# Two recurrences of a convolutional LSTM chain: who rounds the state and who multiplies by the forget gate

## The chip, the cores and the metric

One Trainium2 chip, one of its cores. The metric is the device time of one execution of the whole program in microseconds (us); lower is better. Three executions of the kernel before took 2058.46, 2059.15 and 2060.22 us, median 2059.15.

## What is computed

The input x is 8 images of 48 channels, 64 x 64. Four layers follow one another: an axial filter with attention (L0), two layers of a ConvLSTM that scans the image by rows in both directions (L1, L2), and an inverted residual (L3). The change touches only the scans of L1 and L2. Cut to what matters, one such layer is:

```python
def step(carry, xr):
    h, c = carry
    inp = jnp.concatenate([xr, h], axis=1)
    gates = lax.conv_general_dilated(inp, w_mid, (1,), 'SAME', dimension_numbers=dn) + b[None, :, None]
    i, f, g, o = jnp.split(gates, 4, axis=1)
    c2 = jax.nn.sigmoid(f) * c + jax.nn.sigmoid(i) * jnp.tanh(g)
    h2 = jax.nn.sigmoid(o) * jnp.tanh(c2)
    return ((h2, c2), h2)
hs_f = scan(step, rows)            # 64 rows of 8 x 48 x 64
hs_b = scan(step, rows, reverse=True)
# then: projection of both, batch norm over everything, relu, + x
```

## The kernel before

`build` runs the four layers one after the other; `lstm_scans` is called twice, once for each recurrence. Both directions of a scan are carried in the same tiles, on different partitions: direction d has its own 48 channels (of i and g, and of the state h) on the partitions from `near[d]`, and those of f, o and the cell from `far[d]`, where near and far are 0 and 64 or the other way round. One row of an image batch is 48 channels by BW = 512 columns (8 images of 64). A *turn* below is one direction of one row; a step `s` has two turns, d = 0 and d = 1, and while one direction's gates are computed on the tensor engine, the other's are worked off by the other engines.

The convolution is 14 matmuls of 128 x 112 x 512 for a turn (`chunk`, L712), in two accumulations: `ps[d][0]` holds i and f, `ps[d][1]` g and o. The operands are fp32r, which is rounded, so each of x and h is split into a rounded high part (HI) and the rest (LO). The first two matmuls take part of x (`xc`), the next six x's low part and the high part of h (`xh[..., HI, :]`), the last six the low part of h and a high part.

Each engine has its program written out by hand, and semaphores join them. Nothing plans or reorders. In one turn:

- ScalarE: sigmoid of i and f (L769); then `state_hi` for the other direction, which rounds the new state to the HI part in two halves of 256 columns, each as soon as VectorE has written it (`h_full`, L749); tanh of g in place in PSUM (L773); `copy_state`, the whole state into the LO tile of the other partitions (L756); sigmoid of o (L776); and the tanh of the cell in two halves (L779).
- VectorE: `keep` = sigmoid(f) * cell (L827), i * g in place in PSUM (L830), cell = keep + i*g (L834), the state `hs` = sigmoid(o) * tanh(cell) in two halves (L841), and after direction 1 the rounding of a later row of x (`split_hi`, L819).
- GpSimd: `split_lo`, the low part of x (L685), and `state_lo`, the low part of the state (L676), which waits for `h_hi`. Both are 48 x 512.
- PE waits for `h_hi` ahead of the middle six matmuls and for `h_copy` and `h_lo` ahead of the last six.
- SyncE only issues DMAs: loads of rows of x and their spreading over partitions.

`cell`, `tanh_c` and the gates lie in PSUM; `gate_if`, `gate_o`, `keep`, `hs`, `xh` and `xs` in SBUF. GpSimd reads and writes SBUF tiles only.

Of the kernel before, what the change touches and what calls it, by code (L numbers as in the profile page):

```python
# [13 lines left out]
P = 128  # L14
HALF = 64
HB = B // 2
# [516 lines left out]
def lstm_scans(nc, D, hs, rows_in, weights, tag):  # L533
# [12 lines left out]
    with ctx:  # L546
# [3 lines left out]
        def sb(name, shape, dt=F32):  # L550
            return ctx.enter_context(nc.sbuf_tensor(name + tag, shape, dt))
# [18 lines left out]
        begun = sb("begun", [P, 10])  # L570


        cell = ctx.enter_context(nc.psum_tensor("cell" + tag, [P, BW], F32))
# [17 lines left out]
        kept = [sem(f"kept{d}") for d in range(2)]  # L591
        added = [sem(f"added{d}") for d in range(2)]
        cells = [sem(f"cells{d}") for d in range(2)]
        h_hi = [sem(f"h_hi{d}") for d in range(2)]
# [10 lines left out]
        def inner(ap):  # L605

            return padded(ap)[:, :, 1:W + 1]

        def wide(ap):

            return ap.rearrange("p (b w) -> p b w", b=B)

# [4 lines left out]
        with nc.Block() as block:  # L617
# [49 lines left out]
            @block.gpsimd  # L667
            def _(pool):
                pool.memset(xs[:, :, :].bitcast(F32), 0.0).then_inc(cleared, 1)

                def state_lo(t, row, d, s):

                    n = near[d]
                    pool.wait_ge(h_hi[d], t + 2)
                    whole = hs[n:n + C, bass.ds(row, 1), :].rearrange("p a (b w) -> p (a b) w", b=B)
                    pool.tensor_tensor(inner(xh[n:n + C, d, 1 - s, LO, :]), whole,  # L676
                                       inner(xh[n:n + C, d, 1 - s, HI, :]).bitcast(F32), ALU.subtract).then_inc(h_lo[d], 1)

                def split_lo(t, d, s):

                    f = far[d]
                    pool.wait_ge(x_hi, t + 1)
                    if not (isinstance(t, int) and t < 2):
                        pool.wait_ge(gates[d][1], t - 1)
                    pool.tensor_tensor(inner(xh[f:f + C, d, s, HI, :]), wide(xf[f:f + C, s, :]),  # L685
                                       inner(x_rows(s, slice(f, f + C))).bitcast(F32), ALU.subtract).then_inc(x_lo[d], 1)
                pool.wait_ge(cleared, 3)
                pool.wait_ge(xf_cleared, 1)
                for s in range(2):
                    for d in range(2):  # L690
                        split_lo(s, d, s)

                def step(k, last=False):
                    for s in range(2):
                        for d in range(2):
                            if not last:
                                split_lo(2 * k + (s + 2), d, s)
                            if not last or s == 0:
                                state_lo(2 * k + s, 2 * k + s if d == 0 else k * -2 + (H - 1 - s), d, s)
                with pool.Fori(0, H // 2 - 1) as k:  # L700
                    step(k)
                step(H // 2 - 1, last=True)

            @block.tensor
            def _(pe):
                pe.wait_ge(w_ready, 4)
                pe.wait_ge(cleared, 3)
                with pe.Fori(0, H // 2) as k:
                    for s in range(2):
                        for d in range(2):  # L710
# [11 lines left out]
                            pe.wait_ge(h_hi[d], 2 * k + (s + 1))  # L722
# [11 lines left out]
            def _(act):  # L734
                act.wait_ge(cleared, 3)
                for d in range(2):
                    act.wait_ge(h_hi[d], 1)
                    act.wait_ge(cells[d], 1)
# [5 lines left out]
                def state_hi(t, row, d, s):  # L744

                    n = near[d]
                    for j, part in enumerate(parts):
                        act.wait_ge(h_full[d], t * 2 + (j + 1))
                        hi = nc.scalar.activation(padded(xh[n:n + C, d, s, HI, :])[:, j * HB:(j + 1) * HB, 1:W + 1],  # L749
                                                  state(row, d)[:, part].rearrange("p (b w) -> p b w", b=HB), ACT.Copy)  # L750
                    hi.then_inc(h_hi[d], 1)
# [6 lines left out]
                def step(k, first=False, last=False):  # L758
                    for s in range(2):
                        for d in range(2):  # L760
# [9 lines left out]
                            if some:  # L770
                                state_hi(earlier, row, 1 - d, slot)
                            act.wait_ge(gates[d][1], 2 * k + (s + 1))
# [14 lines left out]
            def _(dve):  # L787
# [19 lines left out]
                for d in range(2):  # L807
                    for i, first in enumerate((h_hi[d], h_lo[d], h_copy[d], sig_if[d], sig_o[d])):
                        nc.vector.memset(begun[:, 5 * d + i:5 * d + i + 1], 0.0).then_inc(first, 1)
# [11 lines left out]
                def step(k, more=2):  # L821
                    for s in range(2):
                        for d in range(2):
# [3 lines left out]
                            nc.vector.tensor_tensor(keep[n:n + C, :], gate_if[f:f + C, d, :], cell[f:f + C, :],  # L827
                                                    ALU.mult).then_inc(kept[d], 1)
# [3 lines left out]
                            dve.wait_ge(kept[d], 2 * k + (s + 1))  # L832
                            dve.wait_ge(added[d], 2 * k + (s + 1))
                            nc.vector.tensor_tensor(cell[f:f + C, :], keep[n:n + C, :], ps[d][1][n:n + C, :], ALU.add  # L834
                                                    ).then_inc(cells[d], 1)
                            dve.wait_ge(sig_o[d], 2 * k + (s + 2))
# [6 lines left out]
                        if s < more:  # L843
                            split_hi(2 * k + (s + 3), 1 - s)
# [5 lines left out]
                step(H // 2 - 1, more=0)  # L850
# [732 lines left out]
```

## Time and profile before

| | us |
|---|---|
| median of three executions | 2059.15 |
| lowest, highest | 2058.46, 2060.22 |
| the profiled execution, its own time | 2065.48 |
| its span in the profile | 2063.5 |
| PE, ScalarE (ACT), VectorE (DVE), GpSimd (POOL) busy | 1656.2, 1198.6, 1257.3, 637.5 |
| first and last keep product (L827) of the two recurrences | 297.2, 1470.6 |

How to read it: a profile is one execution, with the busy time of each engine, the groups of instructions by line with what ended the idle time before them, and a timeline. PE is the tensor engine's matmuls and PEld its weight loads, ACT is ScalarE, DVE is VectorE, POOL is GpSimd, SP is SyncE. In a row, `out<-in` names the tiles, and a name such as `xh_l` stands for the tile of both recurrences. PEclk is the clock that was granted to the tensor engine as a share of its full speed. The busy time of an engine counts over stages that have different limits, so the recurrences are read on their own.

### The profile page before, as it was taken

How to read it: one execution, taken by the hardware profiler on the slowest of the kernel's cores; microseconds unless marked ns; L12 is line 12 of the kernel's file. 1: busy time of each engine (PE TensorE's matmuls, PEld its weight loads, DVE VectorE, ACT ScalarE, POOL GpSimd, SP SyncE). 2: the span in 40 equal slices, each digit the busy share in tenths (PEclk: the TensorE clock that was granted, in tenths of full speed). 3: DMA queues.
4: the chain of work that ended last, by engine and by line, in shares of the span. 5: the costliest groups of instructions: out<-in, count | busy, mean ns of one | idle time of the engine just before them, and what ended most of it. 6: DMA issues, size and time to landing. Idle time of an engine off the chain costs nothing. (4 is left out here: it accounts for less than half of the span.)

```text
span 2063.5 us, 45378 instructions
## 1 busy us (share of the span) xinstructions
PE 1656.2 (80%) x15282; PEld 993.8 (48%) x15282; DVE 1257.3 (61%) x2182; ACT 1198.6 (58%) x2461; POOL 637.5 (31%) x577
## 2 busy tenths in 40 slices
PE   6979238888888887606888888888726999999999
PEld 5545125555555555204555555555403455555555
DVE  5538957777777777455777777777664233333334
ACT  1115218888888888345888888888661232222220
POOL 2010025555555554204555555555200000000000
PEclk9989669999999999757999999999966999999999
DMA  1769356666666664855767776776492001110100
GB/s 62 253 202 216 97 125 105 106 107 105 106 106 106 106 106 68 137 164 95 106 106 106 106 107 105 106 106 107 68 192 53 18 19 32 33 33 18 33 18 26
DMA packets 132283, 199.69 MB, mean 97 GB/s; under 512 B 28528, under 2 KB 47824, under 8 KB 131920
## 3 DMA queue, kind: packets, MB, share of 16 engines
q1 hardware_dynamic: 132176, 198.08, 52.0%
q8 instruction: 89, 1.46, 0.3%
q14 instruction: 18, 0.15, 0.0%
HBM read 73.72 MB, written 37.75 MB: 54 GB/s over the span
## 5 line engine op out<-in xcount | busy, mean ns | idle before, releaser
L712 PE MATMUL gates_l<-xh_l,w_l 128*112 128x512 f32 x3072 | 796.2, 408 | 138.4 <-ACT xh_l L749 138.4
L712 PEld LDWEIGHTS gates_l<-xh_l,w_l 128*112 128x112 f32 x3072 | 511.6, 176 | 423.4 <-issue 285.4
L676 POOL TENSOR_TENSOR xh_l<-hs,xh_l 48x512 fp32r<-48x512 f32 x252 | 301.3, 1196 | 453.1 <-ACT xh_l L749 453.1
L685 POOL TENSOR_TENSOR xh_l<-xf_l,xs_l 48x512 fp32r<-48x512 f32 x256 | 306.0, 1195 | 47.5 <-DVE xs_l L819 47.0
L1259 PE MATMUL b_dw<-b_hid,b_diag 32*32 32x512 f32 x9120 | 313.7, 601 | 0.0
L841 DVE TENSOR_TENSOR hs<-gate_o_l,tanh_c_l 48x256 f32 (+1 forms) x512 | 193.2, 416 | 146.4 <-ACT tanh_c_l L779 146.4
L712 PE MATMUL gates_l<-xc_l,w_l 128*112 128x512 f32 x512 | 165.0, 404 | 144.9 <-DMA xc_l<-xs_l 138.5
L1259 PEld LDWEIGHTS b_dw<-b_hid,b_diag 32*32 32x32 f32 x9120 | 188.0, 103 | 114.4 <-issue 47.4
L830 DVE TENSOR_TENSOR gates_l<-gate_if_l,gates_l 48x512 f32<-48x512 f32 x256 | 178.1, 696 | 87.9 <-ACT gates_l L773 84.0
L779 ACT ACTIVATE tanh_c_l<-cell_l 48x256 f32<-48x256 f32 x512 | 158.1, 342 | 104.7 <-DVE cell_l L834 104.7
L769 ACT ACTIVATE gate_if_l<-gates_l 112x512 f32<-112x512 f32 x256 | 151.2, 590 | 105.2 <-PE gates_l L712 102.0
L1327 ACT ACTIVATE b_h<-b_dw,b_bias_r 128x512 f32<-128x512 f32 x64 | 40.5, 684 | 284.8 <-PE b_dw L1259 284.8
L834 DVE TENSOR_TENSOR cell_l<-keep_l,gates_l 48x512 f32<-48x512 f32 x256 | 178.3, 696 | 26.7
L749 ACT ACTIVATE xh_l<-hs 48x256 fp32r (+1 forms) x504 | 181.6, 407 | 7.9
L827 DVE TENSOR_TENSOR keep_l<-gate_if_l,cell_l 48x512 f32<-48x512 f32 x256 | 175.4, 685 | 10.7 <-ACT gate_if_l L769 1.6
L1371 DVE TENSOR_SCALAR b_h<-b_dw,b_bias_r 128x512 f32<-128x512 f32 x64 | 45.1, 747 | 220.2 <-PE b_dw L1259 220.2
L712 PEld LDWEIGHTS gates_l<-xc_l,w_l 128*112 128x112 f32 x512 | 89.6, 176 | 178.4 <-issue 146.2
L756 ACT ACTIVATE xh_l<-hs 48x512 fp32r (+1 forms) x252 | 159.1, 631 | 6.1
L776 ACT ACTIVATE gate_o_l<-gates_l 48x512 f32<-48x512 f32 x256 | 151.9, 593 | 6.2
L773 ACT ACTIVATE gates_l<-gates_l 48x512 f32<-48x512 f32 x256 | 145.7, 569 | 3.2
L1321 ACT ACTIVATE b_hid<-b_ex,b_bias_h 128x512 f32<-128x512 f32 x116 | 73.8, 689 | 87.6 <-PE b_ex L1231 87.6
L1231 PE MATMUL b_ex<-b_xs,b_w1s 48*128 48x512 f32 x240 | 72.1, 679 | 54.5 <-DMA b_xs<-rows 50.3
(146 smaller groups left out, 1289.5 us busy)
## 6 DMA issues: line engine op xcount, KB each, us to landing
xc_l<-xs_l SPq DMA_DIRECT2D x512, 99.0 KB, 3.0
xh_l<-xs_l SPq DMA_DIRECT2D x512, 66.0 KB, 2.4
xf_l<-rows SPq DMA_DIRECT2D x256, 96.0 KB, 2.1
hs<-rows SPq DMA_DIRECT2D x32, 384.0 KB, 10.2
rows<-hs SPq DMA_DIRECT2D x32, 384.0 KB, 4.9
xr<-in_x_rows SPq DMA_DIRECT2D x24, 256.0 KB, 2.7
xc<-in_x_cols SPq DMA_DIRECT2D x24, 256.0 KB, 2.9
mixed<-stage SPq DMA_DIRECT2D x24, 256.0 KB, 3.0
```

Source lines behind the costliest of these rows:

```text
L676: pool.tensor_tensor(inner(xh[n:n + C, d, 1 - s, LO, :]), whole, inner(xh[n:n + C, d, 1 - s, HI, :]).bitcast(F32), ALU.subtract).then_inc( ...
L685: pool.tensor_tensor(inner(xh[f:f + C, d, s, HI, :]), wide(xf[f:f + C, s, :]), inner(x_rows(s, slice(f, f + C))).bitcast(F32), ALU.subtrac ...
L712: return nc.tensor.matmul(ps[d][m][0:K, :], w[:, d, q, m, :], padded(tile)[:, :, lo:lo + W], start=first, stop=last)
L749: hi = nc.scalar.activation(padded(xh[n:n + C, d, s, HI, :])[:, j * HB:(j + 1) * HB, 1:W + 1], state(row, d)[:, part].rearrange("p (b w) - ...
L756: nc.scalar.activation(inner(xh[f:f + C, d, s, LO, :]), wide(state(row, d)), ACT.Copy).then_inc(h_copy[d], 1)
L776: nc.scalar.activation(gate_o[f:f + C, d, :], ps[d][1][f:f + C, :], ACT.Sigmoid).then_inc(sig_o[d], 1)
L779: nc.scalar.activation(tanh_c[f:f + C, j, 0:PART], cell[f:f + C, part], ACT.Tanh).then_inc(tanhs[d], 1)
L827: nc.vector.tensor_tensor(keep[n:n + C, :], gate_if[f:f + C, d, :], cell[f:f + C, :], ALU.mult).then_inc(kept[d], 1)
L830: nc.vector.tensor_tensor(ps[d][1][n:n + C, :], gate_if[n:n + C, d, :], ps[d][1][n:n + C, :], ALU.mult).then_inc(added[d], 1)
L834: nc.vector.tensor_tensor(cell[f:f + C, :], keep[n:n + C, :], ps[d][1][n:n + C, :], ALU.add).then_inc(cells[d], 1)
L841: nc.vector.tensor_tensor(whole[:, part], gate_o[f:f + C, d, part], tanh_c[f:f + C, j, 0:PART], ALU.mult).then_inc(h_full[d], 1)
L1259: mm = nc.tensor.matmul(dw[r][j * Q:(j + 1) * Q, :], diag[i * Q:(i + 1) * Q, g, 3 * dy + 3 + dx, :], hid[g][i * Q:(i + 1) * Q, y % RING, : ...
```

## The change

Within `lstm_scans`:

- `state_hi` on ScalarE rounds only the first half of the state (`ACT_HALF`). VectorE copies the second half (`DVE_HALF`) itself, behind its two products L841, with a wait on its own result and a one-column memset ahead of the copy. `h_hi` becomes two semaphores, and who waited for one waits for both (PE, GpSimd). ScalarE waits for the second half of the state ahead of its tanh of g.
- The forget product is halved: VectorE makes the first 256 columns, GpSimd the second (`keep_cell`), placed on GpSimd between `split_lo` and `state_lo`. VectorE waits for both halves before it adds. `keep` is written on the cell's own partitions.
- `cell` moves from PSUM to SBUF.
- `split_hi` on VectorE moves: in direction 1 from behind L841 to between the cell's sum and the wait for the sigmoid of o.

```diff
         keep = sb("keep", [P, BW])
-        begun = sb("begun", [P, 10])
-
-
-        cell = ctx.enter_context(nc.psum_tensor("cell" + tag, [P, BW], F32))
+        cell = sb("cell", [P, BW])
+        begun = sb("begun", [P, 13])
...
                 def state_lo(t, row, d, s):
 
                     n = near[d]
-                    pool.wait_ge(h_hi[d], t + 2)
+                    pool.wait_ge(h_hi[d][0], t + 2)
+                    pool.wait_ge(h_hi[d][1], t + 2)
                     whole = hs[n:n + C, bass.ds(row, 1), :].rearrange("p a (b w) -> p (a b) w", b=B)
                     pool.tensor_tensor(inner(xh[n:n + C, d, 1 - s, LO, :]), whole,
                                        inner(xh[n:n + C, d, 1 - s, HI, :]).bitcast(F32), ALU.subtract).then_inc(h_lo[d], 1)
+
+                def keep_cell(t, d):
+
+                    f = far[d]
+                    pool.wait_ge(sig_if[d], t + 2)
+                    pool.wait_ge(cells[d], t + 1)
+                    pool.tensor_tensor(keep[f:f + C, parts[1]], gate_if[f:f + C, d, parts[1]], cell[f:f + C, parts[1]],
+                                       ALU.mult).then_inc(kept[d][1], 1)
...
+                keep_cell(0, 0)
 
                 def step(k, last=False):
                     for s in range(2):
                         for d in range(2):
                             if not last:
                                 split_lo(2 * k + (s + 2), d, s)
+                            if not (last and s == d == 1):
+                                keep_cell(2 * k + (s + d), 1 - d)
...
-                            pe.wait_ge(h_hi[d], 2 * k + (s + 1))
+                            pe.wait_ge(h_hi[d][0], 2 * k + (s + 1))
+                            pe.wait_ge(h_hi[d][1], 2 * k + (s + 1))
...
-                    for j, part in enumerate(parts):
-                        act.wait_ge(h_full[d], t * 2 + (j + 1))
-                        hi = nc.scalar.activation(padded(xh[n:n + C, d, s, HI, :])[:, j * HB:(j + 1) * HB, 1:W + 1],
-                                                  state(row, d)[:, part].rearrange("p (b w) -> p b w", b=HB), ACT.Copy)
-                    hi.then_inc(h_hi[d], 1)
+                    act.wait_ge(h_full[d], t * 2 + 1)
+                    nc.scalar.activation(half(xh[n:n + C, d, s, HI, :], ACT_HALF), state(row, d)[:, parts[ACT_HALF]].rearrange("p (b w) -> p b w", b=HB),
+                                         ACT.Copy).then_inc(h_hi[d][ACT_HALF], 1)
...
+                            if some:
+                                act.wait_ge(h_full[1 - d], earlier * 2 + 2)
...
                         for d in range(2):
                             n, f = near[d], far[d]
                             dve.wait_ge(sig_if[d], 2 * k + (s + 2))
                             dve.wait_ge(cells[d], 2 * k + (s + 1))
-                            nc.vector.tensor_tensor(keep[n:n + C, :], gate_if[f:f + C, d, :], cell[f:f + C, :],
-                                                    ALU.mult).then_inc(kept[d], 1)
+                            nc.vector.tensor_tensor(keep[f:f + C, parts[0]], gate_if[f:f + C, d, parts[0]], cell[f:f + C, parts[0]],
+                                                    ALU.mult).then_inc(kept[d][0], 1)
                             dve.wait_ge(tanh_g[d], 2 * k + (s + 1))
                             nc.vector.tensor_tensor(ps[d][1][n:n + C, :], gate_if[n:n + C, d, :], ps[d][1][n:n + C, :],
                                                     ALU.mult).then_inc(added[d], 1)
-                            dve.wait_ge(kept[d], 2 * k + (s + 1))
+                            for j in range(2):
+                                dve.wait_ge(kept[d][j], 2 * k + (s + 1))
                             dve.wait_ge(added[d], 2 * k + (s + 1))
-                            nc.vector.tensor_tensor(cell[f:f + C, :], keep[n:n + C, :], ps[d][1][n:n + C, :], ALU.add
+                            nc.vector.tensor_tensor(cell[f:f + C, :], keep[f:f + C, :], ps[d][1][n:n + C, :], ALU.add
                                                     ).then_inc(cells[d], 1)
+                            if d == 1 and s < more:
+                                split_hi(2 * k + (s + 3), 1 - s)
...
-                        if s < more:
-                            split_hi(2 * k + (s + 3), 1 - s)
+                            if not (last and s == 1):
+                                dve.wait_ge(h_full[d], 4 * k + (2 * s + DVE_HALF + 1))
+                                nc.vector.memset(begun[:, 12:13], 0.0)
+                                nc.vector.tensor_copy(half(xh[n:n + C, d, 1 - s, HI, :], DVE_HALF), whole[:, parts[DVE_HALF]].rearrange("p (b w) -> p b w", b=HB)
+                                                      ).then_inc(h_hi[d][DVE_HALF], 1)
```

The diff is cut to its core; left out are semaphore lists and `half(ap, j)`, which takes half j of the 8 images of a padded tile. Where code is written in another order, two places show it. On GpSimd, the body of its loop over rows, first half (`split_lo` and `state_lo` write `xh`; `ISA` and `REGISTER_ALU` are waits and address arithmetic). Before:

```order
L684 REGISTER_ALU
L685 TENSOR_TENSOR xh_l<-xf_l,xs_l 48x8x64
L674 REGISTER_ALU
L676 ISA
L676 TENSOR_TENSOR xh_l<-hs,xh_l 48x8x64
L685 TENSOR_TENSOR xh_l<-xf_l,xs_l 48x8x64
L676 ISA
L676 TENSOR_TENSOR xh_l<-hs,xh_l 48x8x64
```

and with the change:

```order
L699 REGISTER_ALU
L700 TENSOR_TENSOR xh_l<-xf_l,xs_l 48x8x64
L689 REGISTER_ALU
L691 TENSOR_TENSOR keep_l<-gate_if_l,cell_l 48x256
L683 ISA
L683 TENSOR_TENSOR xh_l<-hs,xh_l 48x8x64
L700 TENSOR_TENSOR xh_l<-xf_l,xs_l 48x8x64
L691 TENSOR_TENSOR keep_l<-gate_if_l,cell_l 48x256
L683 ISA
L683 TENSOR_TENSOR xh_l<-hs,xh_l 48x8x64
```

One instruction of 256 columns now stands ahead of each `state_lo`. On VectorE, direction 1 at the end of its loop body, from the forget product on (`xs` is the rounded row of x). Before:

```order
L827 TENSOR_TENSOR keep_l<-gate_if_l,cell_l 48x512
L830 TENSOR_TENSOR gates_l<-gate_if_l,gates_l 48x512
L834 TENSOR_TENSOR cell_l<-keep_l,gates_l 48x512
L841 ISA
L841 TENSOR_TENSOR hs<-gate_o_l,tanh_c_l 48x256
L841 ISA
L841 TENSOR_TENSOR hs<-gate_o_l,tanh_c_l 48x256
L813 ISA
L817 REGISTER_ALU
L819 CAST xs_l<-xf_l 112x8x64
```

and with the change:

```order
L846 TENSOR_TENSOR keep_l<-gate_if_l,cell_l 48x256
L849 TENSOR_TENSOR gates_l<-gate_if_l,gates_l 48x512
L854 TENSOR_TENSOR cell_l<-keep_l,gates_l 48x512
L832 ISA
L836 REGISTER_ALU
L838 CAST xs_l<-xf_l 112x8x64
L863 ISA
L863 TENSOR_TENSOR hs<-gate_o_l,tanh_c_l 48x256
L863 ISA
L863 TENSOR_TENSOR hs<-gate_o_l,tanh_c_l 48x256
L867 MEMSET begun_l 128x1
L868 COPY xh_l<-hs 48x4x64
```

The CAST of x stands ahead of the two products that write `hs`, no longer behind them, and a memset and a copy into `xh` follow them.

## Rows read from the trace of the kernel before

**Rows 1.** The page's totals: busy us (share of the span) xinstructions, by engine.
```profile
PE 1656.2 (80%) x15282; PEld 993.8 (48%) x15282; DVE 1257.3 (61%) x2182; ACT 1198.6 (58%) x2461; POOL 637.5 (31%) x577
```

**Rows 2.** Windows, 400 to 800 us: busy us (xinstructions) of each engine, then clock and DMA.
```profile
core 0: us, PE busy (x) PEld busy (x) DVE busy (x) ACT busy (x) POOL busy (x), PEclk, DMA share, GB/s
400.00:800.00 400.00, 346.06 (x1361) 226.06 (x1360) 295.60 (x534) 353.85 (x779) 228.38 (x195) 1.00 0.69 106
```

**Rows 3.** Groups in 400 to 800 us: busy us, mean ns | idle before, releaser.
```profile
L841 DVE TENSOR_TENSOR hs<-gate_o_l,tanh_c_l 48x256 f32 x192 | 72.4, 416 | 55.4 <-ACT tanh_c_l L779 55.4
...
L834 DVE TENSOR_TENSOR cell_l<-keep_l,gates_l 48x512 f32<-48x512 f32 x97 | 67.6, 697 | 10.1
...
L827 DVE TENSOR_TENSOR keep_l<-gate_if_l,cell_l 48x512 f32<-48x512 f32 x97 | 66.4, 685 | 3.6
...
L756 ACT ACTIVATE xh_l<-hs 48x512 fp32r x97 | 61.2, 631 | 2.3
L779 ACT ACTIVATE tanh_c_l<-cell_l 48x256 f32<-48x256 f32 x196 | 60.5, 342 | 36.4 <-DVE cell_l L834 36.4
...
L776 ACT ACTIVATE gate_o_l<-gates_l 48x512 f32<-48x512 f32 x97 | 57.6, 594 | 2.4
```

**Rows 4.** Timeline from 799 us: start, us, engine, line, operation [idle before <-releaser].
```profile
799.77 0.58 ACT L769 ACTIVATE gate_if_l<-gates_l 112x512 f32<-112x512 f32 x1
...
800.38 0.72 ACT L749 ACTIVATE xh_l<-hs 48x256 fp32r x2
800.45 0.43 DVE L819 CAST xs_l<-xf_l 112x512 fp32r<-112x512 f32 x1
...
801.00 0.57 ACT L773 ACTIVATE gates_l<-gates_l 48x512 f32<-48x512 f32 x1
...
801.30 1.19 POOL L676 TENSOR_TENSOR xh_l<-hs,xh_l 48x512 fp32r<-48x512 f32 x1 [1.70 <-ACT xh_l L749]
...
803.80 0.60 ACT L769 ACTIVATE gate_if_l<-gates_l 112x512 f32<-112x512 f32 x1
...
804.42 0.72 ACT L749 ACTIVATE xh_l<-hs 48x256 fp32r x2
...
805.17 0.57 ACT L773 ACTIVATE gates_l<-gates_l 48x512 f32<-48x512 f32 x1
...
805.29 3.11 PE L712 MATMUL gates_l<-xh_l,w_l 128*112 128x512 f32 x12 [0.48 <-ACT xh_l L749]
805.33 1.19 POOL L676 TENSOR_TENSOR xh_l<-hs,xh_l 48x512 fp32r<-48x512 f32 x1 [1.68 <-ACT xh_l L749]
...
805.77 0.70 DVE L830 TENSOR_TENSOR gates_l<-gate_if_l,gates_l 48x512 f32<-48x512 f32 x1 [0.66 <-ACT gates_l L773]
...
806.58 0.70 DVE L834 TENSOR_TENSOR cell_l<-keep_l,gates_l 48x512 f32<-48x512 f32 x1
...
807.31 0.61 ACT L779 ACTIVATE tanh_c_l<-cell_l 48x256 f32<-48x256 f32 x2 [0.30 <-DVE cell_l L834]
807.76 0.74 DVE L841 TENSOR_TENSOR hs<-gate_o_l,tanh_c_l 48x256 f32<-48x256 f32 x2 [0.48 <-ACT tanh_c_l L779]
807.85 0.58 ACT L769 ACTIVATE gate_if_l<-gates_l 112x512 f32<-112x512 f32 x1
```

**Rows 5.** Single lines of VectorE: duration ns min/median/max, first and last start, forms.
```profile
L819 DVE CAST xs_l<-xf_l x128: 421/429/431, 281.0 to 1450.5; 112x512 fp32r<-112x512 f32 x128
...
L213 DVE COPY fx<-hs x96: 209/220/223, 38.0 to 127.4; 64x128 f32 x64, 64x128 f32<-64x128 f32 x32
...
L809 DVE MEMSET begun_l<- x20: 59/59/59, 280.8 to 933.1; 128x1 f32 x20
```

**Rows 6.** Timeline of GpSimd from 840 us, columns as in rows 4.
```profile
840.94 1.30 POOL L950 TENSOR_TENSOR b_diag<-b_eye,b_wds 128x288 f32<-128x288 f32 x2
```

**Rows 7.** Timeline of the program's first 17 us, GpSimd and VectorE, same columns.
```profile
1.14 13.74 POOL L157 MEMSET hs<- 32x16384 f32 x1
...
4.00 10.96 DVE L184 CAST dist<-disti 64x127 f32<-64x127 int32 x1
...
15.51 0.22 DVE L191 TENSOR_SCALAR dist<-dist 64x127 f32<-64x127 f32 x1
```

More of the change, by code:

```diff
@@ L590, in lstm_scans @@
         tanhs = [sem(f"tanhs{d}") for d in range(2)]
-        kept = [sem(f"kept{d}") for d in range(2)]
+        kept = [[sem(f"kept{d}_half{j}") for j in range(2)] for d in range(2)]
         added = [sem(f"added{d}") for d in range(2)]
         cells = [sem(f"cells{d}") for d in range(2)]
-        h_hi = [sem(f"h_hi{d}") for d in range(2)]
+        h_hi = [[sem(f"h_hi{d}_half{j}") for j in range(2)] for d in range(2)]
         h_copy = [sem(f"h_copy{d}") for d in range(2)]
@@ L611, in wide, with half @@
             return ap.rearrange("p (b w) -> p b w", b=B)
+        ACT_HALF, DVE_HALF = 0, 1
+        def half(ap, j):
+            return padded(ap)[:, j * HB:(j + 1) * HB, 1:W + 1]
         def x_rows(r, rows):
@@ L736, in _ @@
                 for d in range(2):
-                    act.wait_ge(h_hi[d], 1)
+                    act.wait_ge(h_hi[d][0], 1)
                     act.wait_ge(cells[d], 1)
@@ L807, in _ @@
                 for d in range(2):
-                    for i, first in enumerate((h_hi[d], h_lo[d], h_copy[d], sig_if[d], sig_o[d])):
-                        nc.vector.memset(begun[:, 5 * d + i:5 * d + i + 1], 0.0).then_inc(first, 1)
+                    for i, first in enumerate((*h_hi[d], h_lo[d], h_copy[d], sig_if[d], sig_o[d])):
+                        nc.vector.memset(begun[:, 6 * d + i:6 * d + i + 1], 0.0).then_inc(first, 1)
                 def split_hi(t, r):
@@ L819, in split_hi, with step @@
                     nc.vector.tensor_copy(inner(x_rows(r, slice(0, K))), wide(xf[0:K, r, :])).then_inc(x_hi, 1)
-                def step(k, more=2):
+                def step(k, more=2, last=False):
                     for s in range(2):
@@ L849, in _ @@
                 step(H // 2 - 2, more=1)
-                step(H // 2 - 1, more=0)
+                step(H // 2 - 1, more=0, last=True)
 class ResidualConstants:
```

## The prediction

> **What bounds the kernel now.** I read the page's totals first, then the two recurrences by stretch, then one stretch turn by turn. The totals say little [rows 1]: the tensor engine is busy 80% of the span, but over stages of different kinds. In a stretch of the first recurrence the clock is 1.00 of full, PE is busy 346 of 400 us, ScalarE 354, VectorE 296, GpSimd 228 [rows 2]: nobody is full. Who waits for whom tells why: ScalarE idles before the cell's tanh and always on VectorE's cell (L834), 36.4 us in 400 [rows 3], and PE idles before the matmuls on the state on ScalarE's rounding (L749), 0.48 us each time [rows 4]. That is a ring, and the timeline gives its links [rows 4]. A "turn" is one direction of one row; L819, once for two turns, has run 128 times [rows 5], so there are 256 turns, 128 in each recurrence. Take T = 803.80, the start of the sigmoid of i and f (L769). Then L749 twice from 804.42, tanh of g (L773) 805.17, product i*g (L830) 805.77, cell (L834) 806.58, tanh of the cell (L779) 807.31, next sigmoid 807.85. The links are 0.62 + 0.75 + 0.60 + 0.81 + 0.73 + 0.54 = 4.05 us. Over two turns, 799.77 to 807.85, it is 4.04, the value I use. VectorE's forget product (L827), the low half of the state on GpSimd (L676) and PE lie beside this ring.
>
> **The change, part by part, if no engine disturbs another.**
> *ScalarE* loses the second L749. The pair takes 0.62 from its start to the next ScalarE instruction in the turn at 800.38 [rows 4], so one is 0.31. The ScalarE ring becomes 4.04 - 0.31 = 3.73.
> *VectorE* gets, behind the two products L841, a wait on its own result, a 1-column memset and the copy of the second half, and its forget product shrinks to 256 columns. Its ring from one tanh of the cell to the next: from the tanh's start to the first L841 0.45 (807.31 to 807.76), plus 0.04 because the cell is now read from SBUF (the 512-column ScalarE instruction is 631 ns from SBUF to SBUF in L756 and 594 from PSUM to SBUF in L776 [rows 3]); the two L841 0.74, a wait on its own result 0.11 (L830 ends 806.47, L834 starts 806.58), the memset 0.06 [rows 5]; the copy 0.29; the half product 0.42 as L841 of the same size [rows 3], plus 0.03; then 0.81 and 0.73 as now. Sum 0.49 + 0.91 + 0.32 + 0.45 + 0.81 + 0.73 = 3.71. The copy's 0.29 has no row; 64x128 takes 220 ns and 112x512 429 [rows 5], which bracket it, and a line between them gives 0.29. The CAST of x (L819, 0.43) moves into VectorE's wait for the tanh, which is 0.45 to 0.49 long: nothing, while that wait covers it; without cover it costs 0.43 in every second turn.
> *GpSimd* gets half the forget product ahead of the low half of the state. Two instructions of 288 columns take 1.30 [rows 6], so 256 columns take 0.58. Asked for at T + 0.60 + 0.19 (GpSimd starts 0.19 after its releaser: 805.14 to 805.33), so from 0.78 to 1.36 after T; state_lo, 1.20 long, to 2.56; split_lo, as large, to 3.76. PE needs 0.15 after a release, and 2.56 from its first state matmul (805.29) to the next sigmoid (807.85), of which the first six of twelve take half of 3.11; so state_lo leads to the next sigmoid at 2.56 + 0.15 + 1.01 = 3.72.
> For VectorE's own write of the cell to SBUF I add nothing: L834 takes 697 ns into PSUM and L827, as wide, 685 into SBUF [rows 3]. PE's busy time alone is 346 of 400 us [rows 2], 3.50 of a turn of 4.04. So three rings end within 0.02 of one another, with PE's own work 0.2 below them. Undisturbed the turn is 3.73, worth 256 x 0.31 = 79 us. But nothing has slack: whatever delays VectorE or GpSimd by more than 0.02 is paid.
>
> **What speaks against it.** At the start of the program GpSimd fills a tile from 1.14 to 14.88, and VectorE's SBUF-to-SBUF CAST of 127 columns, begun at 4.00, ends at 14.96 [rows 7]. A TENSOR_SCALAR of the same 64x127, once GpSimd is idle, takes 0.22. So a VectorE copy waits for the GpSimd instruction that is running, and goes on 0.08 after it. By this the sum that I forecast from is the blocked one. The Trainium skill, page "SBUF — State Buffer", section "Who interferes with whom", says the same in general: a VectorE copy or cast in a two-port mode and a GpSimd instruction take one shared port pair for a whole instruction, and the later one fully blocks. By that rule the trace agrees with the sum below; without it the sum is the 3.73 above.
> In the kernel before, this costs nothing. L819 starts at 800.45 with GpSimd idle until 801.30 [rows 4] and takes 421 to 431 ns in all 128 cases [rows 5]. L830 runs beside state_lo (805.77 against 805.33 to 806.52) at its usual 0.70: with one operand in PSUM it is not held up.
> After the change two kinds of copies meet a busy GpSimd:
> (a) The CAST, in the turns of direction 1. VectorE asks for it once the cell is written, at 0.62 + 0.31 + 0.60 + 0.81 + 0.70 + 0.03 = 3.07 after T. GpSimd's split_lo runs from 2.56 to 3.76. The CAST then starts at 3.84, ends at 4.27, and the first L841, due at 3.07 + 0.49 = 3.56, is 0.71 late.
> (b) The copy of the state, every turn, asked for at -0.54 + 0.49 + 0.91 = 0.86 after T (the tanh starts 0.54 before T, then the terms of VectorE's ring), while GpSimd's half product is asked for at 0.78. If GpSimd is first, the copy waits until 1.44, 0.58 late. If VectorE is first, by as much as one late release, GpSimd starts at about 1.15, all its later work moves by 0.37, and the CAST of (a) becomes about 1.1 late.
> Two turns are 2 x 3.73 = 7.46. With (a) alone, 8.17: 4.09 a turn, +12 us. With (a) and VectorE first in (b), about 8.57: 4.29, +63. With (a) and GpSimd first in one of the two turns (in the turn behind the CAST, VectorE is so late that GpSimd is through), 8.75: 4.38, +87. I take 4.25, between these, as the order of (b) will not be the same throughout: 256 x (4.25 - 4.04) = **+54 us**.
> Everything outside the recurrences is unchanged: the three memsets more are 0.06 each [rows 5]. The sum is 2065.5 + 54 = 2119 for a profiled execution; the median of the runs is 2059.15, 0.3% below that execution, so I forecast 2113.
>
> **The rivals.**
> A, it is faster: GpSimd's arithmetic doesn't hold VectorE up. The row that shows the block has a GpSimd MEMSET, which only writes, for 13.74 us; L676 and L685 also compute and might hold the port only in short pieces. Against it: the CAST waited to the very end of that instruction. The turn is then 3.73, 79 us less: 1980. It decides if CAST and copy show some 0.43 and 0.29 beside a busy GpSimd.
> B, only the forget product is blocked: with the cell in SBUF its VectorE half has two SBUF operands, which no instruction in these recurrences had. It is asked for at 0.86 + 0.32 = 1.18, GpSimd's half ends at 1.36: 0.26 late with the restart, 3.97 to 4.03 a turn, 2041 to 2056. No row here has such a VectorE instruction beside GpSimd. The Trainium skill, the same page and section, states that a VectorE instruction with two SBUF inputs contends with a GpSimd instruction that reads SBUF. Under the blocked copies it would add little, since the copy ahead has waited for the same instruction.
> C, a partial block (GpSimd lets go within its instruction), which lands about halfway between 3.73 and 4.25, near 4.0 a turn: 2040 to 2075.
> DMA queues are none: their waits are all at the start, and two turns' loads keep their place and number.
>
> **How the numbers follow.** Blocked copies 0.64, its own range 2071 to 2150. A 0.16, B 0.12, C 0.08. About 0.2% (4 us) is what a measurement can tell from no change. Slower: 0.64 and 0.02 of C, 0.66. Faster: A, 0.10 of B, 0.03 of C, 0.29. Same: 0.05. The range has to reach down to A to leave out less than 2 in 10: 1976 to 2155.
>
> **What would show it.** Right: L819 after the change far over 0.43, about 1.2, in nearly every case, ending 0.08 behind a GpSimd instruction; the rounding copy at 0.29 or near 0.85 by turns; uneven turns, direction 1's late; ScalarE's wait for the cell above the 0.37 of now (36.4 us in 98 turns [rows 3]); ScalarE with one L749 a turn. Wrong: CAST at 0.43 with split_lo running through it, turns of 3.73 alike (A), or the 48x256 product alone lengthened (B). Not priced: longer turns leave PE idler than its 87% of now [rows 2]; should the granted clock fall below 1.00 within the recurrences, the matmuls would take their place in the ring.

## The result, and the profile after

| | before | with the change |
|---|---|---|
| median of five executions, us | 2060.22 | 2081.95 |
| lowest, highest | 2058.46, 2067.93 | 2079.47, 2083.66 |
| ratio over the runs, 95% interval | | 1.0087 (1.0068 to 1.0106) |
| the profiled execution, its span | 2065.48, 2063.5 | 2080.05, 2077.7 |

The kernel is slower: by 0.87%, or 18 us, by the ratio, and the two medians are 22 us apart. I had forecast slower, by 54 us. In the two profiled executions the recurrences, from their first sigmoid of i and f to their last, grew from 528.1 and 526.1 us to 538.8 and 534.2, 18.8 us together; the stretch between them happened to be 4.0 us shorter. The page of the changed kernel gives its totals and groups (line, engine, operation, tiles, count | busy us, mean ns | idle us before, releaser):

```profile
PE 1668.7 (80%) x15282; PEld 982.5 (47%) x15282; DVE 1401.6 (67%) x2690; ACT 1144.4 (55%) x2209; POOL 833.9 (40%) x833
...
L683 POOL TENSOR_TENSOR xh_l<-hs,xh_l 48x512 fp32r<-48x512 f32 x252 | 309.6, 1229 | 99.5 <-DVE xh_l L868 99.5
...
L691 POOL TENSOR_TENSOR keep_l<-gate_if_l,cell_l 48x256 f32<-48x256 f32 x256 | 187.9, 734 | 196.2 <-ACT gate_if_l L786 196.2
L798 ACT ACTIVATE tanh_c_l<-cell_l 48x256 f32<-48x256 f32 x512 | 176.5, 375 | 142.4 <-DVE cell_l L854 142.4
...
L868 DVE CAST xh_l<-hs 48x256 fp32r (+1 forms) x252 | 143.6, 570 | 3.4
```

Against [rows 1], ScalarE has lost 54 us of work, VectorE has 144 more and GpSimd 196 more, of which its half product, 734 ns each, is 188. `state_lo` (L683) now waits for VectorE's copy, no longer for ScalarE's rounding. The same stretch as [rows 2], then groups of it as in [rows 3]:

```profile
400.00:800.00 400.00, 344.71 (x1331) 217.37 (x1330) 344.27 (x713) 325.50 (x666) 296.83 (x286) 1.00 0.68 104
```

```profile
L798 ACT ACTIVATE tanh_c_l<-cell_l 48x256 f32<-48x256 f32 x190 | 65.5, 375 | 51.0 <-DVE cell_l L854 51.0
...
L868 DVE CAST xh_l<-hs 48x256 fp32r x95 | 55.1, 580 | 1.3
...
L838 DVE CAST xs_l<-xf_l 112x512 fp32r<-112x512 f32 x47 | 50.2, 1069 | 0.0
...
L846 DVE TENSOR_TENSOR keep_l<-gate_if_l,cell_l 48x256 f32<-48x256 f32 x95 | 39.3, 414 | 4.2 <-issue 4.2
```

ScalarE is now busy 325 of 400 us (it was 354), at the same clock of 1.00. What it won it waits away: 51.0 us ahead of 190 tanh of the cell (0.54 a turn), where it was 36.4 [rows 3]. The CAST of x takes 1069 ns on average; it was 429 [rows 5]. VectorE's new copy (L868, shown as CAST) takes 580. Single instructions of these lines, ns min/median/max:

```profile
L838 DVE CAST xs_l<-xf_l x128: 421/1067/1083, 280.8 to 1463.4; 112x512 fp32r<-112x512 f32 x128
...
L868 DVE CAST xh_l<-hs x252: 284/340/843, 300.4 to 1481.3; 48x256 fp32r x120, 48x256 fp32r<-48x256 f32 x6
...
L846 DVE TENSOR_TENSOR keep_l<-gate_if_l,cell_l x256: 406/416/951, 297.0 to 1485.3; 48x256 f32<-48x256 f32 x128
```

The timeline shows when they are long (start, us, engine, line, operation [idle before <-releaser]):

```profile
598.39 1.20 POOL L700 TENSOR_TENSOR xh_l<-xf_l,xs_l 48x512 fp32r<-48x512 f32 x1
...
598.80 1.07 DVE L838 CAST xs_l<-xf_l 112x512 fp32r<-112x512 f32 x1
...
598.92 0.69 ACT L798 ACTIVATE tanh_c_l<-cell_l 48x256 f32<-48x256 f32 x2 [0.57 <-DVE cell_l L854]
599.55 0.60 ACT L786 ACTIVATE gate_if_l<-gates_l 112x512 f32<-112x512 f32 x1
...
599.90 0.75 DVE L863 TENSOR_TENSOR hs<-gate_o_l,tanh_c_l 48x256 f32 x2
...
600.22 0.73 POOL L691 TENSOR_TENSOR keep_l<-gate_if_l,cell_l 48x256 f32<-48x256 f32 x1 [0.63 <-ACT gate_if_l L786]
...
600.79 0.31 DVE L868 CAST xh_l<-hs 48x256 fp32r x1
...
601.29 0.42 DVE L846 TENSOR_TENSOR keep_l<-gate_if_l,cell_l 48x256 f32<-48x256 f32 x1 [0.19 <-issue]
601.37 1.41 POOL L683 TENSOR_TENSOR xh_l<-hs,xh_l 48x512 fp32r<-48x512 f32 x1 [0.42 <-DVE xh_l L868]
...
603.29 0.69 ACT L798 ACTIVATE tanh_c_l<-cell_l 48x256 f32<-48x256 f32 x2 [0.64 <-DVE cell_l L854]
603.81 0.76 DVE L863 TENSOR_TENSOR hs<-gate_o_l,tanh_c_l 48x256 f32 x2 [0.56 <-ACT tanh_c_l L798]
604.00 0.60 ACT L786 ACTIVATE gate_if_l<-gates_l 112x512 f32<-112x512 f32 x1
...
604.68 0.72 POOL L691 TENSOR_TENSOR keep_l<-gate_if_l,cell_l 48x256 f32<-48x256 f32 x1 [0.74 <-ACT gate_if_l L786]
604.72 0.83 DVE L868 CAST xh_l<-hs 48x256 fp32r x1
...
606.95 1.19 POOL L700 TENSOR_TENSOR xh_l<-xf_l,xs_l 48x512 fp32r<-48x512 f32 x1
...
607.36 1.06 DVE L838 CAST xs_l<-xf_l 112x512 fp32r<-112x512 f32 x1
...
608.12 0.60 ACT L786 ACTIVATE gate_if_l<-gates_l 112x512 f32<-112x512 f32 x1
```

The reader is to see four things. The CAST begins while GpSimd's `split_lo` (L700) runs, 598.39 to 599.59 and 606.95 to 608.14, and ends 0.28 behind it both times. The copy takes 0.31 at 600.79, where GpSimd's half product (600.22 to 600.95) is almost through, and 0.83 at 604.72, where that had begun 0.04 before; both times it ends 0.15 behind it. And the first product L863 comes 0.98 after the tanh's start behind a CAST (598.92 to 599.90), 0.52 otherwise (603.29 to 603.81): the CAST makes it 0.46 late. The sigmoids start at 599.55, 604.00, 608.12, then 612.29 and 616.40: turns of 4.45, 4.12, 4.17 and 4.11, on average 4.21.

The fourth is the turn of 4.45. VectorE's half product (L846) starts at 601.29, 0.19 after the copy ahead of it has ended, where it otherwise follows at once. `state_lo`, begun beside it at 601.37, then takes 1.41 for 1.19. This pause stands 29 times in the first recurrence, each time between the last instruction of one pass of VectorE's loop and the first of the next; 30 passes have 29 such places, and the eight turns written out behind the loop have none. In the second recurrence it is 0.03 to 0.08, and the turn 4.31. Against the 4.17 of the other turn behind a CAST, that is 29 x 0.28 + 29 x 0.14 = 12 us, most of the 18.8 by which the recurrences grew. In the kernel before, the turns at these places take 4.19 and 4.17 against 4.18.

A third meeting, the last rows of the recurrence:

```profile
800.58 1.19 POOL L700 TENSOR_TENSOR xh_l<-xf_l,xs_l 48x512 fp32r<-48x512 f32 x1
...
801.00 1.07 DVE L838 CAST xs_l<-xf_l 112x512 fp32r<-112x512 f32 x1
...
806.60 0.88 POOL L691 TENSOR_TENSOR keep_l<-gate_if_l,cell_l 48x256 f32<-48x256 f32 x1 [0.66 <-ACT gate_if_l L786]
...
806.82 0.95 DVE L846 TENSOR_TENSOR keep_l<-gate_if_l,cell_l 48x256 f32<-48x256 f32 x1
```

Here VectorE's copy was not held up (606.61 to 606.89), and its half of the forget product, both operands in SBUF, met GpSimd's half: 0.95 where 0.41 is usual, while GpSimd's took 0.88 for 0.73. GpSimd's ended at 807.48, 0.59 behind the copy, and VectorE's at 807.77, 0.29 behind GpSimd's: the ends stand as if each had waited for the one ahead. This agrees with the Trainium skill, page "SBUF — State Buffer", section "Who interferes with whom", where a VectorE instruction with two SBUF inputs contends with a GpSimd instruction that reads SBUF.

### The profile page after: what moved, and what is told of

Its sections match the earlier page's. It is cut to its first block and busy times, and to the rows that moved or that the text cites. A ratio compares the mean times of both kernels' runs of the same rounds, so it can differ in the third digit from the quotient of the medians.

```text
span 2077.7 us, 46410 instructions
## 1 busy us (share of the span) xinstructions
PE 1668.7 (80%) x15282; PEld 982.5 (47%) x15282; DVE 1401.6 (67%) x2690; ACT 1144.4 (55%) x2209; POOL 833.9 (40%) x833
## 5 line engine op out<-in xcount | busy, mean ns | idle before, releaser
L730 PE MATMUL gates_l<-xh_l,w_l 128*112 128x512 f32 x3072 | 811.6, 411 | 143.5 <-DVE xh_l L868 141.6
L730 PEld LDWEIGHTS gates_l<-xh_l,w_l 128*112 128x112 f32 x3072 | 502.7, 176 | 452.0 <-issue 312.8
L683 POOL TENSOR_TENSOR xh_l<-hs,xh_l 48x512 fp32r<-48x512 f32 x252 | 309.6, 1229 | 99.5 <-DVE xh_l L868 99.5
L700 POOL TENSOR_TENSOR xh_l<-xf_l,xs_l 48x512 fp32r<-48x512 f32 x256 | 306.4, 1197 | 33.4 <-DVE xs_l L838 32.9
L691 POOL TENSOR_TENSOR keep_l<-gate_if_l,cell_l 48x256 f32<-48x256 f32 x256 | 187.9, 734 | 196.2 <-ACT gate_if_l L786 196.2
L798 ACT ACTIVATE tanh_c_l<-cell_l 48x256 f32<-48x256 f32 x512 | 176.5, 375 | 142.4 <-DVE cell_l L854 142.4
L863 DVE TENSOR_TENSOR hs<-gate_o_l,tanh_c_l 48x256 f32 (+1 forms) x512 | 193.1, 416 | 78.1 <-ACT tanh_c_l L798 74.3
L838 DVE CAST xs_l<-xf_l 112x512 fp32r<-112x512 f32 x128 | 132.5, 1037 | 28.7 <-DMA xf_l<-rows 28.7
L868 DVE CAST xh_l<-hs 48x256 fp32r (+1 forms) x252 | 143.6, 570 | 3.4
L767 ACT ACTIVATE xh_l<-hs 48x256 fp32r (+1 forms) x252 | 104.8, 416 | 42.4 <-DVE hs L863 39.1
```

The source lines that it names most:

```text
L691: pool.tensor_tensor(keep[f:f + C, parts[1]], gate_if[f:f + C, d, parts[1]], cell[f:f + C, parts[1]], ALU.mult).then_inc(kept[d][1], 1)
L730: return nc.tensor.matmul(ps[d][m][0:K, :], w[:, d, q, m, :], padded(tile)[:, :, lo:lo + W], start=first, stop=last)
L798: nc.scalar.activation(tanh_c[f:f + C, j, 0:PART], cell[f:f + C, part], ACT.Tanh).then_inc(tanhs[d], 1)
L863: nc.vector.tensor_tensor(whole[:, part], gate_o[f:f + C, d, part], tanh_c[f:f + C, j, 0:PART], ALU.mult).then_inc(h_full[d], 1)
```

## The experiments

Two theories stood at the start. **P**: GpSimd's instructions block VectorE's copies and its product of two SBUF operands, and this gives back what ScalarE won. **L**: VectorE's chain and the tanh that reads SBUF are simply longer, and the blocks lie in slack. Ratios are to the kernel before, run on the same chip beside each (medians 2062.22, 2063.05 and 2065.36 us in three groups); each ratio is uncertain by 0.1 to 0.3%, so a difference of two ratios by a little more. Turns are distances of the sigmoids of i and f near 600 us. Groups are of 400 to 800 us unless another stretch is named.

### Without the copies' second port

**a7**: the change, but the CAST of x is a product with a column of ones in PSUM.

```diff
+        one = ctx.enter_context(nc.psum_tensor("one" + tag, [P, 1], F32))
...
+                nc.vector.memset(one[:, :], 1.0)
...
-                    nc.vector.tensor_copy(inner(x_rows(r, slice(0, K))), wide(xf[0:K, r, :])).then_inc(x_hi, 1)
+                    nc.vector.tensor_tensor(inner(x_rows(r, slice(0, K))), wide(xf[0:K, r, :]), one[0:K, :].unsqueeze(2).broadcast_to([K, B, W]), ALU.mult).then_inc(x_hi, 1)
```

> The changed kernel, but VectorE rounds the row of x by a product with a column of ones in PSUM (one SBUF operand, so one port) instead of a CAST. Theory P (VectorE's two-port and two-SBUF-operand instructions are blocked by GpSimd, and that gives back the gain): the instruction takes about 0.70 us in every case, not 1.07, though split_lo runs beside it; the two turns together get up to 0.37 us shorter, 2035 to 2075 us, and the less, the more the state's copy or the half product run into GpSimd instead. Theory L (the changed kernel is slow because VectorE's chain is longer and the cell's tanh reads SBUF; the blocks lie in slack): 2080, no change.

2068.84 us, ratio 1.0036 (1.0023 to 1.0048). Groups, 400 to 800 us:

```profile
L870 DVE CAST xh_l<-hs 48x256 fp32r x96 | 68.4, 713 | 1.3
...
L840 DVE TENSOR_TENSOR xs_l<-xf_l,one_l 112x512 fp32r<-112x512 f32 x48 | 33.1, 690 | 1.5
```

The product takes 690 ns whatever GpSimd does. It is 260 longer than a free CAST, and the kernel is still 0.5% faster than the change. The gain is small since VectorE, now earlier, meets GpSimd's half product in its copy instead: 713 on average, not 580. Turns are 4.11 and 4.18. Read turn by turn, 4.45, 4.12, 4.17 and 4.11 have become 4.18, 4.11, 4.18 and 4.11: only the turn at the loop's edge is shorter, and the pause there is gone. The block of the CAST, taken away alone and at the price of the longer product, gave nothing else back.

**a3**: the change, but wait, memset and copy are replaced by a third product, straight into `xh`.

```diff
-                                dve.wait_ge(h_full[d], 4 * k + (2 * s + DVE_HALF + 1))
-                                nc.vector.memset(begun[:, 12:13], 0.0)
-                                nc.vector.tensor_copy(half(xh[n:n + C, d, 1 - s, HI, :], DVE_HALF), ...
+                                nc.vector.tensor_tensor(half(xh[n:n + C, d, 1 - s, HI, :], DVE_HALF), images(gate_o[f:f + C, d, parts[DVE_HALF]]),
+                                                        images(tanh_c[f:f + C, DVE_HALF, 0:PART]), ALU.mult).then_inc(h_hi[d][DVE_HALF], 1)
```

> The changed kernel, but the second half of the rounded state is written by a third product sigmoid(o)*tanh(cell) straight into the rounded tile (one operand in PSUM, no wait on its own result, no memset) instead of memset and copy. P: the product takes 0.42 always, where the copy took 0.28 to 0.84; some 0.1 us a turn less, 2050 to 2075 us. L: about the same length of chain (0.42 for 0.11 + 0.06 + 0.29), 2080 within 5.

2041.62 us, ratio 0.9893 (0.9877 to 0.991): faster than before. Groups:

```profile
L850 DVE TENSOR_TENSOR keep_l<-gate_if_l,cell_l 48x256 f32<-48x256 f32 x100 | 58.3, 583 | 3.1
...
L870 DVE TENSOR_TENSOR xh_l<-gate_o_l,tanh_c_l 48x256 fp32r<-48x256 f32 x100 | 41.5, 415 | 0.0
```

One operand is `tanh_c` in PSUM, and the product takes its usual 415 beside GpSimd. A turn gains the block, 0.58 - 0.29 = 0.29, and 0.46 - 0.415 = 0.04 of wait, memset and free copy, and loses 0.17 by the half product next in line, now 583 for 414. By this sum that is 256 x 0.16 = 41 us, and the whole program is 40 us shorter (0.0194 of the time). That they are equal is partly luck: the turns went from 4.21 to 3.91 and 4.12, 0.20 less on average, the pause at the loop's edge being gone here too. In the profiles the two recurrences are 46 us shorter, and the stretches between and behind them 9 us longer.

**a6**: both edits.

> Both of the above: no VectorE instruction of the loop takes two ports; only its half of the forget product still has two SBUF operands. P: turns of 3.90 to 3.97 us, 2025 to 2045 us, faster than the kernel before by over 0.7%. L: 2075 to 2085.

2021.16 us, ratio 0.9795 (0.9779 to 0.9812), a little under the expected range. Groups:

```profile
L688 POOL TENSOR_TENSOR xh_l<-hs,xh_l 48x512 fp32r<-48x512 f32 x101 | 135.0, 1336 | 2.5
...
L852 DVE TENSOR_TENSOR keep_l<-gate_if_l,cell_l 48x256 f32<-48x256 f32 x102 | 61.8, 606 | 3.3
```

Together they are worth 2.9% against the change, more than 0.5 + 1.9: the delay no longer moves from one copy to the other. Turns are 3.91 and 3.95, where a3 still has 4.12 behind its blocked CAST. What is left is the collision of the two half products (606 for 414) and of VectorE's with `state_lo` (1336, usually 1196).

**a9**: a6 with 64 instead of 256 columns in GpSimd's half product. The forget product of the other 192 columns is left out (they stay zero).

```diff
-                    pool.tensor_tensor(keep[f:f + C, parts[1]], gate_if[f:f + C, d, parts[1]], cell[f:f + C, parts[1]],
+                    pool.tensor_tensor(keep[f:f + C, PART:PART + W], gate_if[f:f + C, d, PART:PART + W], cell[f:f + C, PART:PART + W],
```

> The version with both one-port instructions (2021 us), but GpSimd makes only one of its four images of the forget product (64 of 256 columns); for the other three keep stays zero, so the cell forgets there. What is left out is 192 columns of a GpSimd product per turn. If the half product's collision (VectorE's 256 columns take 606 ns on average instead of 414, state_lo on GpSimd 1336 instead of 1196) is on the ring, turns get 0.05 to 0.15 us shorter: 1980 to 2010 us, with VectorE's product at about 0.42. If it lies in slack: 2021 within 4.

2006.70 us, ratio 0.9718 (0.9701 to 0.9734). Groups, 400 to 780 us:

```profile
L688 POOL TENSOR_TENSOR xh_l<-hs,xh_l 48x512 fp32r<-48x512 f32 x97 | 118.4, 1221 | 33.8 <-DVE xh_l L873 22.6 <-ACT xh_l L772 11.2
...
L853 DVE TENSOR_TENSOR keep_l<-gate_if_l,cell_l 48x256 f32<-48x256 f32 x97 | 40.8, 420 | 3.0
...
L696 POOL TENSOR_TENSOR keep_l<-gate_if_l,cell_l 48x64 f32<-48x64 f32 x97 | 30.9, 319 | 83.0 <-ACT gate_if_l L791 83.0
```

The half product is back at 420 and `state_lo` at 1221: collision and length of GpSimd's half together are worth 0.8% of a6 (16 us by the ratios, 14.5 by the medians, which are of different chips), no more. The turns became only about 0.03 shorter (3.90 on average for 3.93), less than the 0.05 to 0.15 that I expected. Which of the two has more of it this run can't say.

### The parts alone, on the kernel before

**e2**: only the cell in SBUF, `keep` on its partitions.

```diff
-        cell = ctx.enter_context(nc.psum_tensor("cell" + tag, [P, BW], F32))
+        cell = sb("cell", [P, BW])
```

> The kernel before with nothing changed but the cell in SBUF (and keep on the cell's partitions). The tanh of the cell should take 375 ns instead of 342, the pair 0.69 instead of 0.61. Both theories: the ring gets 0.06 to 0.08 us a turn longer, 2073 to 2080 us; P adds nothing, as GpSimd is idle while VectorE makes the forget product. If the price of SBUF is hidden: 2060.

2075.75 us, ratio 1.007 (1.0054 to 1.0087). Groups:

```profile
L676 POOL TENSOR_TENSOR xh_l<-hs,xh_l 48x512 fp32r<-48x512 f32 x96 | 128.7, 1340 | 160.7 <-ACT xh_l L749 160.7
...
L779 ACT ACTIVATE tanh_c_l<-cell_l 48x256 f32<-48x256 f32 x192 | 66.2, 375 | 34.2 <-DVE cell_l L834 34.2
```

The tanh reads SBUF in 375 ns instead of 342, twice in a ring; the forget product, now with two SBUF operands, holds `state_lo` up (1340 for 1196), where I had written that P adds nothing. This single part costs 0.7%; how that divides between the tanh and the held-up `state_lo`, the run doesn't say. I had counted the tanh's 0.04 on VectorE's ring alone.

**f3**: only the rounding is split (ScalarE one half, VectorE wait, memset and copy); the CAST stands where it was, the forget product is whole, the cell in PSUM.

> The kernel before with the rounding split alone: ScalarE the first half, VectorE memset and copy for the second; whole forget product on VectorE, cell in PSUM, CAST in its old place behind the copy. VectorE's ring is then 0.45 + 0.91 + 0.32 + 0.72 + 0.81 + 0.73 = 3.94, and the CAST adds 0.46 in every second turn: 4.1 to 4.2 us a turn, 2075 to 2100 us. P and L agree here, GpSimd being idle at the copy. If it is faster than before, VectorE's chain is not what ends the turn.

2092.93 us, ratio 1.0146 (1.0116 to 1.0176), the slowest of all. Groups:

```profile
L787 ACT ACTIVATE tanh_c_l<-cell_l 48x256 f32<-48x256 f32 x188 | 58.0, 342 | 77.1 <-DVE cell_l L842 77.1
...
L854 DVE CAST xh_l<-hs 48x256 fp32r x94 | 27.0, 288 | 1.3
```

No copy is blocked here: 288 ns, and the CAST 429. Yet turns are 3.86 and about 4.65. The 3.86 is shorter than any turn of before; in the other VectorE has products, copy, CAST and the whole forget product in a row, and ScalarE waits 77.1 us in all for the cell. So the first half of L holds too: a longer VectorE chain costs by itself, and the halved forget product and the CAST in the gap pay for more than they cost.

**f1**: only the CAST is moved into the wait for the tanh.

```diff
+                            if d == 1 and s < more:
+                                split_hi(2 * k + (s + 3), 1 - s)
                             dve.wait_ge(sig_o[d], 2 * k + (s + 2))
...
-                        if s < more:
-                            split_hi(2 * k + (s + 3), 1 - s)
```

> The kernel before with the CAST of x moved into VectorE's wait for the tanh, as the change does, and nothing else. In the kernel before split_lo runs there too, from about 2.7 to 3.9 us after the sigmoid of i and f. P: the CAST takes 0.7 to 0.8 us instead of 0.43; the state comes up to 0.2 us late in every second turn, of which ScalarE's slack before it rounds hides most: 2060 to 2075 us. L: 0.43 and 2055 to 2060, since VectorE loses 0.46 us of work behind the state.

2053.80 us, ratio 0.9958 (0.9944 to 0.9973). The CAST's line, ns min/median/max:

```profile
L819 DVE CAST xs_l<-xf_l x128: 422/657/673, 280.3 to 1437.8; 112x512 fp32r<-112x512 f32 x128
```

It is blocked by 0.23 and the kernel is still faster. So the CAST behind the products had not been free in the kernel before. That was against P, and led back to my own base.

**b3**: only that CAST taken off VectorE, as a product with ones on GpSimd behind its other work.

```diff
+                    pool.tensor_tensor(inner(x_rows(r, slice(0, K))), wide(xf[0:K, r, :]), one[0:K, :].unsqueeze(2).broadcast_to([K, B, W]), ALU.mult).then_inc(x_hi, 1)
...
-                        if s < more:
-                            split_hi(2 * k + (s + 3), 1 - s)
```

> The kernel before with only the rounding of x taken from VectorE to GpSimd. The forecast took 4.04 us for a turn of the kernel before, from a stretch where the last rows ran; over the whole recurrence a turn is 4.12, alternately 4.05 and 4.18, and the 4.18 are those with the CAST behind the products. If the CAST is the cause, all turns become about 4.05: 256 x 0.065 = 17 us less, 2042 to 2050 us. If not, 2060.

2045.11 us, ratio 0.9914 (0.9892 to 0.9935). Groups, 400 to 780 us:

```profile
L794 ACT ACTIVATE tanh_c_l<-cell_l 48x256 f32<-48x256 f32 x188 | 58.0, 342 | 27.4 <-DVE cell_l L850 27.4
...
L697 POOL TENSOR_TENSOR xs_l<-xf_l,one_l 112x512 fp32r<-112x512 f32 x47 | 49.0, 1042 | 7.9 <-POOL xh_l L677 7.9
```

All turns are now alike, 4.02 to 4.06, and ScalarE waits 27.4 us for the cell. 256 x (4.12 - 4.04) = 20 us; measured are 18 by the ratio and 20 by the medians, and in the profiles the recurrences are 19 us shorter.

### A faster version

**f5**: the rounding split by a3's third product, a7's product for x in the gap, but cell in PSUM and forget product whole.

> Rounding split with the third product, CAST in the gap as a one-port product, and the cell left in PSUM with the whole forget product on VectorE: nothing two-port and nothing with two SBUF operands is left. VectorE's ring 0.45 + 1.14 + 0.72 + 0.81 + 0.73 = 3.85 and a quarter us more in every second turn: about 3.93 to 3.97, 2035 to 2050 us. Against the version with halved forget product and the cell in SBUF (2021) it tells what that part of the change is worth once the ports are free: about 20 us. If that part is only a burden, this one is the faster, 2005 to 2015.

2030.92 us, ratio 0.9855 (0.9825 to 0.9885), turns 3.78 and 4.17. Against f3 that is 2.9%. Against a6 it lacks 0.6%, with intervals that just don't touch: once no copy is blocked, the halved forget product with its SBUF cell is worth its price: about 12 us, not the 20 that I expected. The range for the time, 2035 to 2050, was missed by 4 us.

**f6**: f5 with the rounding of x on GpSimd, as in b3.

> The same, but the rounding of x goes to GpSimd (a product with one, about 1.2 us in every second turn) and leaves VectorE altogether. VectorE's ring 3.85, ScalarE's 3.73: 3.8 to 3.87 us a turn, 2005 to 2022 us, if GpSimd (6.0 of 7.7 us in two turns) still delivers the low half of the state in time; if not, above 2040.

2011.11 us, ratio 0.9749 (0.9722 to 0.9776). Groups:

```profile
L708 POOL TENSOR_TENSOR xs_l<-xf_l,one_l 112x512 fp32r<-112x512 f32 x49 | 51.1, 1042 | 8.3 <-POOL xh_l L688 8.3
```

Turns of 3.78 and 4.04. This is the fastest version that leaves nothing out, 2.5% below the kernel before and 3.4% below the change. GpSimd's 1042 ns for x stand where it had idled. The average turn is 3.91, above the 3.8 to 3.87 expected.

## Why the prediction came out as it did

**Right: direction and mechanism.** The kernel became slower, and CAST and copy wait for a running GpSimd instruction to its end; the copy has two lengths; ScalarE waits longer for the cell; one L749 fewer brought ScalarE nothing. Taking the second port away (a7, a3, a6) turned +0.9% into -2.0%. Rival A falls: a free CAST is 0.43, it took 1.07. So does C: GpSimd did not let go within an instruction. Rival B exists, but beside the copies: the half product takes 0.95 at most and 0.42 in the median, and 0.61 on average once the copies are out of the way (a6).

**The step that failed: "Over two turns, 799.77 to 807.85, it is 4.04, the value I use".** These are the last rows of the recurrence, written out behind the loop, with the last CAST of x at 800.45. The timeline of the kernel before at 602 us, within the loop:

```profile
601.53 0.61 ACT L779 ACTIVATE tanh_c_l<-cell_l 48x256 f32<-48x256 f32 x2 [0.30 <-DVE cell_l L834]
602.07 0.58 ACT L769 ACTIVATE gate_if_l<-gates_l 112x512 f32<-112x512 f32 x1
602.12 0.74 DVE L841 TENSOR_TENSOR hs<-gate_o_l,tanh_c_l 48x256 f32 x2 [0.63 <-ACT tanh_c_l L779]
...
602.90 0.43 DVE L819 CAST xs_l<-xf_l 112x512 fp32r<-112x512 f32 x1
603.32 0.57 ACT L773 ACTIVATE gates_l<-gates_l 48x512 f32<-48x512 f32 x1
603.36 0.69 DVE L827 TENSOR_TENSOR keep_l<-gate_if_l,cell_l 48x512 f32<-48x512 f32 x1
...
604.08 0.69 DVE L830 TENSOR_TENSOR gates_l<-gate_if_l,gates_l 48x512 f32<-48x512 f32 x1
...
606.25 0.60 ACT L769 ACTIVATE gate_if_l<-gates_l 112x512 f32<-112x512 f32 x1
```

The first L841 comes 0.59 after the tanh's start, where I had read 0.45 (807.31 to 807.76). So the CAST stands at 602.90, 0.83 after the sigmoid's start, at the end 0.68 after it (800.45), and pushes the forget product to 603.36. This ends at 604.05, and i*g begins at 604.08, though its tanh had ended at 603.89. The turn is 606.25 - 602.07 = 4.18; the one without CAST 4.05. The average was 4.12, and my own row had it: 97 turns in 400 us [rows 3] are 4.12 each. b3 shows the difference as 18 to 20 us. Why the first product follows sooner in the rows behind the loop, no run shows. With this base the same 4.25 would have given 256 x 0.13 = +33 instead of +54: of the 32 us that I forecast too much, 21 are the base, and the rest is the 4.25 itself.

**Terms mis-sized, downwards.** (a) The CAST makes the first L863 0.46 late, not 0.71. GpSimd's release came 0.66 after the tanh's start (607.48 to 608.14), about my 0.69; but the CAST then ended 0.28 later, where I had added 0.08 and a whole CAST of 0.43. (b) 0.83 - 0.29 = 0.54 late for 0.58, in one turn of two, as said. Two turns by my sum are then 7.46 + 0.46 + 0.54 = 8.46; measured are 4.45 + 4.12 = 8.57 and 4.17 + 4.11 = 8.28, on average 8.43. That makes 4.21 a turn for my 4.25, and in the second recurrence it is 4.18: 128 x (0.09 + 0.06) = 19 us, as the two profiles have it. That the mean comes so near is luck. It hides a term too small, GpSimd's half product, which takes 0.73 and not 0.58, and two that I lacked: the tanh pair takes 0.69, not 0.61, and the pause at the loop's edge holds 12 of these 19 us. Two turns without that pause are 8.28, 0.18 less than 8.46. Nor does any run show my undisturbed turn of 3.73; with no copy blocked, products in place of CAST and copy, and the rest of the change as it is, a6 takes 3.91 and 3.95.

**What was left open in the forecast.** The clock stayed at 1.00 from 400 to 800 us, and from 930 to 1450 it was 0.98 before and 0.97 after. The cell's write to SBUF costs nothing (687 ns; 697 in [rows 3]). The pause at the loop's edge, ahead of the half product, has nothing but "issue" behind it. Its places, 29 between 30 passes and none behind the loop, point to the loop's jump, but no run takes the jump away, so the cause is argued. In a7, a3 and a6 no such turn stands out, though they jump as often; in e2 (4.24 against 4.18) and f3 (4.71 against 4.61) a smaller one does.

## What to carry to other kernels

Read the length of a ring over a whole period of its loop in the middle of its run, and check it by a count (instructions in a stretch); here the rows written out behind the loop ran faster than the rest. When work moves between VectorE and GpSimd, look at each VectorE copy or cast, and each product with two SBUF operands, for who runs beside it: a product with one operand in PSUM did the same rounding at a fixed price, and writing the rounded result straight from the product made the copy needless. A part that costs alone (the SBUF cell, 0.7%) can pay together with what it makes possible (GpSimd's half of the forget product), once the collisions around it are gone, so try parts together as well as alone. And list the turns one by one: an average of 4.21 hid one turn in four that held most of the loss.

## What the hardware showed that I had not expected

- A blocked copy does not begin anew at the release. It ends 0.28 behind GpSimd's instruction with 512 columns, 0.15 with 256, and 0.08 with 127 [rows 7], while free ones take 0.43 and 0.29: some 0.14 to 0.15 is spent while it waits. Products with two operands in SBUF look alike: VectorE's half ended 0.29 behind GpSimd's (free 0.41), and in e2 `state_lo` ended 1.07 behind VectorE's forget product (598.80 to 599.87; free 1.20).
- A blocked CAST in a gap can be better than a free one in a chain (f1).
- A GpSimd TENSOR_TENSOR (two tiles in, one out) of 48x256 takes 0.73 us, one of 48x64 0.32 and one of 48x512 1.19: by my estimate from these, about 0.2 of each is fixed. Two of 128x288 in 1.30 [rows 6] had let me expect 0.58.
- ScalarE reads 256 columns of SBUF 33 ns slower than of PSUM (375 and 342).
